# Scan layers' set-up: other banks and order for the first projections, one norm moved ahead of an addition, paddings cleared by GpSimd

## The reference

```python
def _mamba_layer(x, W_in, conv_w, conv_b, W_x, W_dt, b_dt, A_log, Dvec, W_out):
    u, z = jnp.split(jnp.einsum('bld,ed->ble', x, W_in), 2, axis=-1)
    u = _silu(_causal_conv1d(u, conv_w, conv_b))          # 4 taps, left padded with 3 zeros
    dt, Bm, Cm = jnp.split(jnp.einsum('bld,rd->blr', u, W_x), [DT_RANK, DT_RANK + D_STATE], axis=-1)
    dt = jax.nn.softplus(jnp.einsum('blr,dr->bld', dt, W_dt) + b_dt)
    y = _selective_scan(u, dt, -jnp.exp(A_log), Bm, Cm, Dvec)   # 16 states for each of 256 channels
    return jnp.einsum('bld,od->blo', y * _silu(z), W_out)
h = _layernorm(x) * (1 + ca) + sa
x = x + ga * (_mamba_layer(_mamba_layer(h, layer 0), layer 1) + h)
```

## Time and profile before

| | us |
|---|---|
| runs | 753.18, 755.59, 757.89 |
| median | 755.59 |
| profiled execution | 753.51 |
| its span, first to last instruction | 751.6 |

### The profile page before, as it was taken

How to read it: one execution, slowest core, us unless ns; L and a number is a source line. 1 busy time by engine, 2 the same in 40 slices (tenths; PEclk the granted TensorE clock), 3 DMA queues, 4 the chain that set the end, 5 groups by cost and what they waited for, 6 DMA issues and landing times. The chain is left out here.

```text
span 751.6 us, 8865 instructions
## 1 busy us (share of the span) xinstructions
PE 634.6 (84%) x2909; PEld 394.8 (53%) x2909; DVE 584.4 (78%) x820; ACT 497.2 (66%) x935; POOL 457.1 (61%) x259
## 2 busy tenths in 40 slices
PE   3955777688699999999988699999999972599992
PEld 2443455433455555555422455565655561499982
DVE  6794897557799999999765799999999958734521
ACT  3643534468999898989568999898989553033320
POOL 0136664100598989889600498989888615358866
PEclk9866788698799999999998699999999975599997
DMA  5000000001132323333001223232332181023323
GB/s 200 0 3 1 1 1 0 1 2 61 53 88 98 99 90 93 98 90 105 31 3 44 58 86 99 97 99 84 100 99 90 52 308 57 3 27 41 40 30 28
DMA packets 30780, 48.05 MB, mean 64 GB/s; under 512 B 3736, under 2 KB 12328, under 8 KB 30224
## 3 DMA queue, kind: packets, MB, share of 16 engines
q1 hardware_dynamic: 25600, 44.45, 18.4%
q0 software_dynamic: 5136, 3.05, 3.7%
HBM read 42.98 MB, written 4.49 MB: 63 GB/s over the span
## 5 line engine op out<-in xcount | busy, mean ns | idle before, releaser
L481 POOL TENSOR_TENSOR hc_all<-hs_all,c_row 128x1024 f32<-128x1024 f32 x87 | 205.0, 2369 | 122.0 <-DVE hs_all L1674 121.2
L1149 PE MATMUL ps<-hc_all,ident 128*128 128x512 f32 x508 | 237.1, 598 | 2.7 <-POOL hc_all L481 2.7
L1674 DVE TENSOR_TENSOR_SCAN hs_all<-da,ps 128x1024 f32<-128x1024 f32 x88 | 197.9, 2270 | 14.1 <-ACT da L811 9.1
L811 ACT ACTIVATE da<-big,a_neg 128x511 f32<-128x511 f32 x256 | 169.3, 709 | 30.7 <-DVE w_ffn L1674 29.1
L1149 PEld LDWEIGHTS ps<-hc_all,ident 128*128 128x128 f32 x508 | 90.2, 192 | 86.9 <-issue 77.0
L481 POOL TENSOR_TENSOR hc_all<-w_ffn,c_row 128x1024 f32<-128x1024 f32 x40 | 94.7, 2368 | 29.7 <-DVE w_ffn L1674 26.5
L1674 DVE TENSOR_TENSOR_SCAN w_ffn<-da,ps 128x1024 f32<-128x1024 f32 x40 | 91.4, 2285 | 3.8 <-ACT da L811 0.9
L1169 PE MATMUL ps<-ident,dbu 128*128 128x128 f32 x464 | 62.2, 279 | 11.2 <-ACT dbu L786 6.0
L1169 PEld LDWEIGHTS ps<-ident,dbu 128*128 128x128 f32 x464 | 54.2, 143 | 25.8 <-issue 18.7
L547 POOL DMA_INDIRECT out<-hc_all,hs_all x32 | 52.2, 1632 | 11.9 <-issue 8.8
L888 ACT ACTIVATE big<-ps,b 128x516 f32<-128x516 f32 x32 | 22.1, 690 | 47.3 <-PE ps L1340 47.3
(11 more groups left out here) (309 smaller groups left out, 1025.5 us busy)
## 6 DMA issues: line engine op xcount, KB each, us to landing
c_row<-c_rows SPq DMA_DIRECT2D x128, 256.0 KB, 3.1
tmpA<-w_in SPq DMA_DIRECT2D x2, 1024.0 KB, 7.2
tmpB<-w_in SPq DMA_DIRECT2D x2, 1024.0 KB, 9.3
x_tok<-x_in SPq DMA_DIRECT2D x2, 512.0 KB, 5.7
out<-x_tok SPq DMA_DIRECT2D x1, 1024.0 KB, 11.9
xm_rows<-xn SPq DMA_DIRECT2D x1, 1024.0 KB, 5.0
w_mod<-w_mod_in SPq DMA_DIRECT2D x2, 384.0 KB, 6.5
w_ffn<-w_ffn_in SPq DMA_DIRECT2D x1, 560.0 KB, 7.7
```

The costliest lines, as they stand in the source:

```text
L481: nc.gpsimd.tensor_tensor(hc[:, n % 4, :, :], hs3[HS_BUF[n]].rearrange("p (i s) -> p i s", i=IC), c_row[:, n % 4, :].unsqueeze(1).to_broad ...
L811: ins = nc.scalar.activation(da[:, n % 2, i, 1:S], dtT[:, b, i, 1:S], ACT.Exp, scale=a_neg[:, l, i, n:n + 1])
L1149: mm = nc.tensor.matmul(ps[:, YS + i, :], ident[:], hc[:, n % 4, i, :], start=(n == 0), stop=(n == NS - 1))
L1674: v.tensor_tensor_scan(hs3[HS_BUF[n]], decay, pair.rearrange("p i s -> p (i s)"), 0.0, ALU.mult, ALU.add).then_inc(c_scan, 1)
```

## The change

- TensorE: u of batch 0 in layer 0 goes to banks 6 and 7, z of batch 0 to banks 4 and 5. The projection of u of batch 0 is ahead of the transposes of batch 2, that of z right behind them, then the transposes of batch 3. The waits follow the new banks. W_x of batch 0 waits for z of batch 0 in both layers. In layer 1, W_x of batch 0 is ahead of u of batch 2.
- VectorE: the norm of batch 2 and the clear of the paddings for layer 0 are ahead of the addition of the last pair.
- GpSimd: clears the paddings for layer 1, at the end of its list for layer 0.
- ScalarE: the load of the silu table is behind the modulation of batch 3 (in the list: behind u of batch 0) and no more ahead of that of batch 2.

```diff
--- before.py
+++ after.py
@@ -159,7 +159,7 @@
         dtT = big[:, 0:IC * T].rearrange("p (b i s) -> p b i s", b=B, i=IC)
         dtuT = big[:, IC * T:2 * IC * T].rearrange("p (b i s) -> p b i s", b=B, i=IC)
         SP = S + KC - 1
-        U_BANK, Z_BANK = [[0, 0, 0, 0], [2, 2, 0, 0]], [[2, 2, 2, 2], [4, 0, 2, 2]]
+        U_BANK, Z_BANK = [[6, 0, 0, 0], [2, 2, 0, 0]], [[4, 2, 2, 2], [4, 0, 2, 2]]
         XD, DTP = [4, 5], [6, 6, 6, 0]
         hs_all = sb("hs_all", [P, 2 * IC * S])
         hs = hs_all[:].rearrange("p (k i s) -> p k i s", k=2, i=IC)
@@ -483,6 +483,10 @@
                                                 ALU.mult).then_inc(c_hc, 1)
                         if (b, n) in DTU_AT:
                             dt_times_u(DTU_AT[b, n])
+                if l + 1 < L:
+                    for k in range(2):
+                        pool.wait_ge(c_sum, NS * B - 2 + 2 * k)
+                        nc.gpsimd.memset(u_pad[:, k, :, 0:KC - 1], 0.0).then_inc(pad_ready, 1)
 
             pool.wait_ge(m_x, B)
             nc.gpsimd.affine_select(out=lower, in_=ones[0:BE, 0:BE], compare_op=ALU.is_ge, fill=0.0, base=-1,
@@ -699,7 +703,6 @@
             modulated_second(0)
             modulated_second(1)
             deviation(2, 3)
-            act.preload_act_table(ACT.Silu)
             modulated_second(2)
             for l in range(L):
                 q = sems[l]
@@ -750,6 +753,7 @@
                         ins.then_inc(q["m_u0"], 1)
                         if (l, b) == (0, 0):
                             modulated_second(B - 1)
+                            act.preload_act_table(ACT.Silu)
                     if b == B + 1:
                         act.wait_ge(b_turn, l + 1)
                         nc.scalar.copy(b_cols[:].rearrange("p t n -> p (t n)"), ps[:, TURN, :]).then_inc(b_ready, 1)
@@ -1060,7 +1064,6 @@
             transposed_second(0)
             down(2 * B - 1)
             transposed_second(1)
-            transposed_second(2)
 
             pe.wait_ge(ld_mamba, 96 + 32 * B)
             def project_in(l, b, half):
@@ -1069,7 +1072,10 @@
                 if l:
                     pe.wait_ge(c_h, b + 1)
                 elif b == 0:
-                    pe.wait_ge(hT_ready, B + 2 * (half + 1))
+                    pe.wait_ge(hT_ready, B + 1)
+                    pe.wait_ge([q_h["q_rounded"], f_x][half], 2 * B)
+                elif b == 1:
+                    pe.wait_ge(hT_ready, B + 2 * ((1 - half) + 2 * half))
                 bank = [U_BANK, Z_BANK][half][l][b]
                 if l and b < 3:
                     if b == 0:
@@ -1080,7 +1086,7 @@
                         pe.wait_ge(q["m_z"], 2)
                     else:
                         pe.wait_ge(q["m_u0"], 2 * b)
-                else:
+                elif l or b > 1:
                     after(pe, q[["m_u0", "m_z"][half]], [2, 1][half] * b)
                 for i in range(IC):
                     mm = nc.tensor.matmul(ps[:, bank + i, :], w_in[:, l, (2 * half + i) * P:(2 * half + i + 1) * P],
@@ -1102,6 +1108,8 @@
                 q = sems[l]
                 if l == 0:
                     project_in(0, 0, 0)
+                    transposed_second(2)
+                    project_in(0, 0, 1)
                     transposed_second(B - 1)
                 def project_dt(b):
                     pe.wait_ge(q["m_dtl"], b + 1)
@@ -1115,24 +1123,26 @@
                 for b in range(B + 1):
                     if b >= 2:
                         project_dt(b - 2)
-                    if b < B and (l, b) != (1, 0):
+                    if b < B and b + l and (l, b) != (1, 0):
                         project_in(l, b, 1)
                     if (l, b) == (1, 1):
                         pe.wait_ge(c_h, B - 1)
                         for part in range(IC + 1):
                             project_out(0, B - 1, part)
-                    if b + 1 < B and (l, b) != (1, 0):
+                    if b + 1 < B and (l, b) not in ((1, 0), (1, 1)):
                         project_in(l, b + 1, 0)
                     if 0 < b <= B:
 
                         pe.wait_ge(q["m_u"], IC * b)
-                        if l and b == 1:
+                        if b == 1:
                             pe.wait_ge(q["m_z"], 1)
                         after(pe, q["m_rows"], b - 2)
                         for i in range(IC):
                             mm = nc.tensor.matmul(ps[0:DR + 2 * NS, XD[(b - 1) % 2], :], w_x[:, l, i, :], uT[:, b - 1, i, :],
                                                   start=(i == 0), stop=(i == IC - 1))
                         mm.then_inc(q["m_xd"], 1)
+                    if (l, b) == (1, 1):
+                        project_in(l, b + 1, 0)
                 pe.wait_ge(q["m_rows"], B)
                 for t in range(TB):
                     mm = nc.tensor.transpose(ps[:, TURN, t * P:(t + 1) * P], bc_all[:, t * P:(t + 1) * P], ident[:])
@@ -1590,11 +1600,13 @@
             second_stats(2)
             inverse(4, 1)
             normalise_batch(1)
+            inverse(4, 2)
+            normalise_batch(2)
+            v.memset(u_pad[:, :, :, 0:KC - 1], 0.0).then_inc(pad_ready, 1)
             add_down(2 * B - 1)
             second_stats(3)
-            for b in range(2, B):
-                inverse(4, b)
-                normalise_batch(b)
+            inverse(4, 3)
+            normalise_batch(3)
             for l in range(L):
                 q = sems[l]
                 def softplus(b, i):
@@ -1610,11 +1622,6 @@
                 if l == 0:
                     dve.wait_ge(a_exp, 1)
                     v.tensor_scalar(a_neg[:], a_neg[:], -1.0, None, ALU.mult).then_inc(a_ready, 1)
-                if l:
-                    dve.wait_ge(c_sum, B * NS - 2)
-                    v.memset(u_pad[:, 0, :, 0:KC - 1], 0.0).then_inc(pad_ready, 1)
-                else:
-                    v.memset(u_pad[:, :, :, 0:KC - 1], 0.0).then_inc(pad_ready, 1)
                 for b in range(B + 1):
                     if b >= 2:
                         positive(b - 2)
@@ -1636,7 +1643,6 @@
                     if l and b == 0:
                         dve.wait_ge(c_sum, NS * B)
                         v.tensor_tensor(y_sb[:], ps[:, YS:YS + IC, :], zT[:, B - 1, :, :], ALU.mult).then_inc(c_y, 1)
-                        v.memset(u_pad[:, 1, :, 0:KC - 1], 0.0).then_inc(pad_ready, 1)
                 dve.wait_ge(q["m_ln"], 3)
                 dve.wait_ge(q["m_pos"], IC)
                 v.tensor_tensor(dtT[:, 0, :, :], dtT[:, 0, :, :], ps[:, LN_FIRST:LN_FIRST + IC, :], ALU.add).then_inc(q["m_dt"], 1)
```

## The result

| | before | after |
|---|---|---|
| median, us | 755.16 (4 runs, 753.18 to 757.89) | 744.83 (4 runs, 741.10 to 747.42) |
| profiled execution, us | 753.51 | 745.24 |
| its span | 751.6 | 743.3 |
| mean granted TensorE clock | 0.896 | 0.907 |

The ratio is 0.9874, with a 95% interval of 0.9836 to 0.9912: 9.5 us faster, between 6.6 and 12.4. The forecast of 749.0 was 6.6 us, at the interval's small end; the measured median of 744.8 lies within the stated 744 to 754, close to its lower end. The kernel after was measured a second time with the experiments: ratio 0.9908 (0.9875 to 0.9942), 6.9 us.

What follows compares the result with a forecast made beforehand. The two set-ups, chains of waits with no engine full, were taken as what the change can shorten. Layer 0's 6.3 - 1.2 = 5.1 us plus layer 1's 1.5 gave 6.6 off the 755.6 median: 749.0 us, range 744 to 754.

Steps and rivals of the forecast that it cites:

- Bounds and stages: Whole span: the diff leaves the full scans alone; the two set-ups are chains of waits, where each microsecond won shortens the span.
- (1) to (4): Layer 0's set-up: earlier norm, new banks and order leave ScalarE last; copy of u of batch 1 comes 6.3 us earlier.
- My price for its move: ScalarE in layer 0's set-up: the table load, no longer covered by a wait, costs 0.6 us more than at its old place.
- (5): Layer 0: a new 2.5 us TensorE pause before u of batch 2 lowers the clock; cost 1.2 us, bounds 0 and 1.7.
- a pattern that moves as a whole: Layer 0's set-up from the copy of u of batch 1 on: depends on nothing earlier, so it starts 6.3 us earlier.
- (6): Layer 1's set-up: GpSimd's padding clear, queued behind its last product by C, delays the path 0.1 us (0.1 to 0.8).
- (7): Layer 1's set-up: W_x of batch 0 ahead of u of batch 2 removes waits; 1.6 us, 1.5 less the clear's delay.
- (8): Layer 1, 397.5 to 400.5 us: low clock under z of batch 3, worth 1.5 us, may stay, go or move; left to range.
- A: Rival, TensorE's clock: no low stretch behind the new pause, perhaps none at 397; gain 7.8 to 9.3 us; chance 0.33.
- C: Rival, layer 0: its lead is lost before the first scan, only layer 1's 1.5 us remain; 754.1 us; chance 0.05.
- D: Rival, set-ups: TensorE falls to 1.2 GHz and stays there through one; slower, over 1% lost at 764 us; chance 0.05.
- B: Rival, set-ups: uncovered table load costs more, or a new wait appears; 1 to 2 us each, 751.6 to 752.6; chance 0.13.

Runs made afterwards that it cites:

- experiment 1: Kernel after with layer 1's parts undone (W_x of batch 0 behind u of batch 2, VectorE clears); ratio to the kernel before 0.9947.
- 6: Kernel after with the silu table loaded at its old place, ahead of batch 2's modulation; ratio to the kernel before 0.9902, 746.0 us.
- 7: Kernel after with the early table load and the silu of z of batch 0 behind batch 1's tap products; ratio to before 0.9887, 746.4 us.
- experiment 4: Kernel after with batch 2's norm behind the addition again; ratio to the kernel before 0.9936, 4.9 us faster.
- experiment 3: Kernel before with only batch 2's norm moved ahead of the addition; ratio to the kernel before 1.0032.
- 5: Kernel after, unchanged, measured and profiled again; ratio to the kernel before 0.9908, 747.1 us.
- 9: Kernel after with dt projections from 128 rows of other weights and data instead of 8; ratio to the kernel before 0.9865, 742.8 us.
- 8: Kernel after with ten idle matmuls in TensorE's pause ahead of u of batch 2 in layer 0; ratio to the kernel before 0.9911, 748.3 us.
- E0: Not a run: the point in every kernel's profile where layer 0's last scan ends.
- 2: Kernel before with layer 1's parts alone (W_x of batch 0 ahead of u of batch 2, GpSimd clears); ratio to the kernel before 0.9955.
- 10: As 7, with idle matmuls filling the waits ahead of layer 0's dt projections of batches 0 to 2; ratio to the kernel before 0.9913, 746.0 us.
- 11: As 7, with dt projections from 128 rows of other weights and data; ratio to the kernel before 0.9848, 741.7 us.

## Why the prediction was right or wrong

**Bounds and stages.** Right. The scans kept their length, and both gains lie in the set-ups.

**(1) to (4), the chain in layer 0.** Right. Forecast 6.3 us for the copy of u of batch 1; measured 6.1 against the start of batch 1's norm (17.16 - 11.08) and 6.1 in experiment 1 (17.16 - 11.04); the other profiles of the kernel before would make it up to 6.8. ScalarE is last, as experiments 6 and 7 show: what is taken off its list comes off A to C. The norm's share within it is 0.9 to 1.1 us (experiment 4); alone, on the old banks, it gave 1.2 (experiment 3). Counted from A, u of batch 0 starts at 2.98 us (137.70 - 134.72) where it was 6.15 (142.64 - 136.49), and the transposes of batch 2, now behind it, at 4.70 where they were 5.24.

**The table load.** It took 1.28 us, at 143.59 in the profile after, 0.02 us behind the end of the modulation and with the silu of z 0.01 us behind its own end. The Trainium skill, page "ScalarE: Activation LUTs", section "What ACT_TABLE_LOAD costs", gives 2.66 us for a switch, a drain of 1.38 included. The trace does not agree: there is no room for a drain on either side of the load. My price for its move, 0.6 us, measured 0.8 to 1.0.

**(5), the clock.** The level does fall in this set-up, but seldom at the place that I named. The pause came, 2.42 us long; the forecast term was 1.2 us, and it was 0 in the profile after and in experiments 1, 5 and 9. The level did fall behind it in experiment 4, at a price of 1.65 us, so the bounds of 0 and 1.7 hold. But filling it (8) or cutting it (7) did not gain anything, since the level falls elsewhere: behind the dt projections, for up to 4.5 us in the stretch C to F0 (five of the eleven profiles with eight rows and no filler ahead of dt). This stretch I had called a pattern that moves as a whole.

**(6), GpSimd's clear.** Right: 0.12 us on the path for a forecast of 0.1.

**(7), W_x first.** Right: the first dt projection starts 1.40 us earlier against E0 (19.12 before, 17.72 after), for a forecast of 1.5.

**(8), the low stretch in layer 1.** This step and the 1.2 us of (5) are the two that mis-sized the sum. I left it in at 1.5 us of its own and gave its going to the range, as if it were drawn. It went, and took 1.36 us with it. TensorE's rows of the profile before at this place:

```profile
395.03 1.98 PE L1111 MATMUL ps<-hs_all,w_dt 8*128 8x512 f32 x4 [0.67 <-ACT hs_all L734]
396.94 3.56 PE L1086 MATMUL ps<-xn,w_in 128*128 128x512 f32 x4
400.42 1.99 PE L1133 MATMUL ps<-tmpA,w_x 128*40 128x512 f32 x4
403.08 1.98 PE L1111 MATMUL ps<-hs_all,w_dt 8*128 8x512 f32 x4 [0.67 <-ACT hs_all L734]
```

The third dt projection followed the second by 8.05 us (395.03 to 403.08), with u at 3.56 us between them, and follows it by 6.69 after (385.71 to 392.40). Four profiles against eight speak against luck: the old order has it, the new one has not.

**The sum.** Forecast 6.3 - 1.2 + 1.5 = 6.6. Measured 6.1 - 0 + 1.4 + 1.36 = 8.8 in the profiles; 9.5 and 6.9 in the times. Of the rivals, A (the clock stays kind, 7.8 to 9.3 us) is what the profile after shows. C and D did not come. Neither did B as I gave it. Alone the parts gave 4.0 and 3.4 us (experiments 1 and 2), 7.4 together, between the two measurements of the whole. Executions with low stretches behind dt may be why the times gave less than the profiles; no profile caught the kernel after in one (the second profile, at 741.9 us, is the fastest of its six executions). By the first measurement the gain lies above the 5 to 7.6 us that I gave the forecast the best chance, by the second inside it: that the median came within the range owes something to the width I had left for A.

**What stays open.** Why the level falls in layer 1's old order every time and in layer 0 in some executions is not settled. With 128 rows there was no fall ahead of the fourth dt projection (9, 11), and in one profile filling the waits did as well (10), though its times show no gain. So the depth of the dt projection and the wait ahead of it may both bear on it; this is argued from three profiles, and their shares are not told apart. Nor is the depth told apart from the data, since 9 and 11 changed both. Nor is it known why moving u of batch 2 spares layer 1. And the stretch M to the end took 129.5 to 135.5 us in kernels that are the same there. GpSimd issues its last gather or scatter 123.8 to 129.7 us behind M, so the difference has arisen by then; what makes it, no run here looked into.

## What to carry to other kernels

When a set-up is a chain over four engines, write the new times for each engine's list before choosing the one to relieve; here a bank and an order freed TensorE, and ScalarE was last at once, with a table load that had lost its cover. Don't take a low stretch of the clock for luck before a second profile, and look at what TensorE did just ahead of it: a shallow matmul behind a wait is a candidate, and a run with full rows gives an estimate of its price. A part of the change can lose alone (the norm, 0.3% slower, just clear of its interval) and pay within the whole, so price parts by stretches of the profile as well as by times, which here varied by 3 to 10 us between the executions of one kernel.

## What the runs showed of the hardware that was not expected

- TensorE's granted level held at 2.4 GHz through a pause of 2.42 us in four profiles (after, 1, 5 and 9) and fell 1.4 us behind one as long in experiment 4. In the kernel before it fell within two such pauses, 0.5 and 0.4 us ahead of their ends.
- With the dt projections at 8 rows the set-up from C to F0 took 31.3 to 36.0 us by kernel and execution; at 128 rows, the same columns and other data, 31.1 and 31.3 us, and the mean granted clock over the span was 0.912 and 0.915 (experiments 9 and 11) where the same kernels with 8 rows had 0.902 and 0.900 (5 and 7).
- The level fell near the fourth dt projection of layer 0 in all twelve profiles with 8 rows, and in experiment 9 with 128.
- A clear of six columns took 0.10 us on GpSimd, the same as one of one column, for 0.06 us on VectorE.
